# Transformer block on one core: attention inputs (batches 1 to 7) and second-FFN inputs (0 to 6) transposed by VectorE in 32x32 blocks and a DMA hop through DRAM, with new orders of work

## The reference

```python
x = x + 0.5 * ffn(layernorm(x))        # ffn: layernorm * gamma + beta, then a 256x256 ternary weight, + bias
x = x + attention(layernorm(x))        # 16 query heads, 4 key/value heads of 128, rotary embedding,
                                       # causal window of 64, softmax, output projection 2048 -> 256, + bias
x = x + 0.5 * ffn(layernorm(x))        # the same ffn once more
```

## Time and profile before

| | us |
|---|---|
| runs, median of 3 (lowest, highest) | 791.79 (791.75, 793.09) |
| the profiled execution, its own time | 793.39 |
| its span in the trace | 790.5 |

### The profile page before, as it was taken

One profiled execution on the slowest core, in us unless ns is written; L12 is line 12 of the kernel. 1 busy time (PEld: TensorE's weight loads), 2 busy tenths in 40 slices (PEclk: granted clock), 3 DMA queues, 4 the chain that ended last, 5 costly groups with the idle time before them and its releaser, 6 DMA issues.

```text
span 790.5 us, 16087 instructions
## 1 busy us (share of the span) xinstructions
PE 778.3 (98%) x5630; PEld 727.2 (92%) x5630; DVE 626.1 (79%) x1321; ACT 469.6 (59%) x1602; POOL 455.7 (58%) x466
## 2 busy tenths in 40 slices
PE   8999999999999999999999999999999999999997
PEld 7688999999999999999999999999999999999996
DVE  5888967988688877888769887688867988688757
ACT  5366665657646565655747556475664657645574
POOL 3778555766446754567536773476635676446443
PEclk9999999999999999999999999999999999999999
DMA  8572324352252423425153242533224452243410
GB/s 300 114 194 59 90 55 120 95 127 48 55 152 63 121 54 89 126 55 120 41 135 94 68 99 49 134 92 97 67 55 121 94 129 45 57 104 68 107 29 27
DMA packets 54352, 74.10 MB, mean 94 GB/s; under 512 B 7168, under 2 KB 30208, under 8 KB 54272
## 3 DMA queue, kind: packets, MB, share of 16 engines
q1 hardware_dynamic: 53712, 72.74, 37.7%
q10 hardware_dynamic: 560, 0.34, 0.2%
HBM read 14.33 MB, written 4.19 MB: 23 GB/s over the span
## 4 chain that ended last, share of the span: by engine, by line
PE 92%; DVE 3%; POOL 2%; DMA 1%; issue 1%; ACT 0%; SPq 0%; DVEq 0%; POOLq 0%
PE job_p L656 33%; PE attn_p L656 22%; PE scores_p L673 13%; PE heads_p L656 11%; PE probsT_p L737 7%; PE job_p L833 4%; PE job_p L817 2%; POOL q_s L1282 1%; DMA x_res<-wo 1%; POOL probs L1271 1%; DMA x_in<-x 0%; DVE parts L1015 0%; DMA rope_swap<-rope_sin 0%; POOL wo_s L1253 0%; DVE rope_sin L934 0%
## 5 line engine op out<-in xcount | busy, mean ns | idle before, releaser
L656 PE MATMUL attn_p<-wo_s,headsT 128*128 128x256 f32 x1536 | 209.2, 286 | 1.0 <-ACT headsT L1175 0.7
L656 PE MATMUL job_p<-xnT,wq_s 128*128 128x512 f32 x768 | 205.3, 403 | 1.2 <-DVE v_s L951 1.1
L656 PEld LDWEIGHTS attn_p<-wo_s,headsT 128*128 128x128 f32 x1536 | 196.5, 191 | 7.0 <-ACT headsT L1175 1.4
L1154 ACT ACTIVATE probs<-scores_p,neg_max 128x96 f32<-128x96 f32 x512 | 167.6, 352 | 51.8 <-DVE neg_max L900 51.6
L1271 POOL TENSOR_TENSOR probs<-probs,inv_sum 128x384 f32<-128x384 f32 x128 | 107.9, 843 | 152.0 <-DVE inv_sum L906 151.9
L1282 POOL TENSOR_TENSOR q_s<-q_s,rope_swap 128x512 f32<-128x512 f32 x128 | 164.3, 1291 | 52.3 <-DMA rope_swap<-rope_sin 52.2
L1175 ACT ACTIVATE headsT<-heads_p,columns_s 128x512 fp32r<-128x512 f32 x128 | 88.0, 688 | 140.9 <-PE heads_p L656 140.5
L656 PEld LDWEIGHTS job_p<-xnT,wq_s 128*128 128x128 f32 x768 | 135.8, 189 | 26.6 <-DVE v_s L951 1.7
L934 DVE SCALAR_TENSOR_TENSOR rope_sin<-job_p,columns_s,rope_t 128x512 f32<-128x512 f32 x160 | 118.9, 743 | 21.1 <-PE job_p L656 19.9
L673 PE MATMUL scores_p<-k_s,q_s 128*128 128x96 f32 (+2 forms) x1024 | 131.6, 272 | 0.3 <-POOL q_s L1282 0.2
L673 PEld LDWEIGHTS scores_p<-k_s,q_s 128*128 128x128 f32 x1024 | 126.5, 192 | 3.4 <-POOL q_s L1282 1.1
(11 more groups left out here) (96 smaller groups left out, 972.7 us busy)
## 6 DMA issues: line engine op xcount, KB each, us to landing
rope_swap<-rope_sin SPq DMA_DIRECT2D x320, 128.0 KB, 2.3
v_odd<-v_s SPq DMA_DIRECT2D x64, 192.0 KB, 3.3
x_in<-x SPq DMA_DIRECT2D x15, 256.0 KB, 4.2
out<-x_res SPq DMA_DIRECT2D x15, 256.0 KB, 2.5
x_tr<-x_transposed SPq DMA_DIRECT2D x7, 512.0 KB, 5.3
q_s<-wq SPq DMA_DIRECT2D x3, 512.0 KB, 10.1
q_s<-wo SPq DMA_DIRECT2D x2, 512.0 KB, 10.6
x_res<-wo SPq DMA_DIRECT2D x2, 512.0 KB, 4.8
```

What stands on the lines that cost most here:

```text
L656: mm = nc.tensor.matmul(dst, a(p), b(q), start=clears and i == 0, stop=len(pairs) == 1, skip_group_check=True)
L1154: ins = nc.scalar.activation(probs[:, i, k, 0:REACH], scores_p[i][:, k, 0:REACH], ACT.Exp, bias=neg_max[:, i, k:k + 1], accum_out=row_sum[ ...
```

## The change

Fourteen pairs of halves are transposed in another way: XT of batches 1 to 7 and YT2 (written YT..p) of batches 0 to 6. Their `job_p` transposes on TensorE are gone. Instead
- the normalization writes y as runs of 32 elements in another order;
- "turn" (YT2) and "aturn" (XT), one VectorE instruction over 128x1024 float32 in place, transposes every 32x32 block;
- "send" and "asend" on SP copy all of y (512 KB) to a DRAM tensor; "land" and "aland" wait for that, and bring it back by four DMAs of 128 KB into `x_tr`, which puts the blocks on their partitions;
- ScalarE and VectorE make high and low parts from `x_tr` instead of PSUM: for XT one operation of 128x512 per chunk e instead of per half; for YT2 VectorE's low parts are cut into 128 columns.

`x_tr` now has two more tenants per batch, so `loadt` moved behind YT..p. All five tables are written anew. The lines of middle batches around the attention input, and the core of the rest:

```diff
 TENSOR middle
-        W4c T5c S7c K3c O4c Q12c W5c T6c Q13c S8c O5c FO0n W6c T7c
-        S9c Q14c FO1n O6c W7c T8c Q15c S10c O7c W8c XT0n T9c XT1n S11c
-        O8c K0n W9c T10c Q0n S12c O9c W10c T11c V00n S13c Q1n O10c W11c
+        T3c S5c Q9c Q10c O2c W3c FO0p T4c S6c Q11c O3c W4c T5c FO1p
+        O4c S7c K3c Q12c W5c T6c S8c Q13c O5c W6c T7c S9c FO0n FO1n
+        Q14c O6c Q15c W7c T8c S10c O7c W8c T9c O8c W9c S11c T10c O9c
+        W10c S12c T11c S13c K0n Q0n O10c W11c V00n T12c S14c Q1n Q2n O11c
 TENSOR first
+        W6c S8c FO0n T7c FO1n Q14c O6c W7c S9c Q15c T8c O7c W8c S10c
+        O8c T9c S11c W9c T10c O9c S12c W10c T11c S13c K0n O10c Q0n W11c
 VECTOR middle
-        Q12c probsT6c heads5c max8c Q13c YT1n FO0n heads6c max9c inv8c Q14c probsT7c FO1n astats0n
-        astats1n heads7c inv9c probsT8c Q15c max10c XT0n heads8c max11c XT1n inv10c probsT9c K0n inv11c
+        heads15p Q6c probsT0c Q7c evac1p max2c stats1p heads0c K2c max3c turn0p inv2c probsT1c Q8c
+        K3c Q12c inv7c heads5c max8c probsT6c Q13c inv8c heads6c max9c FO0n FO1n astats0n astats1n
+        Q14c probsT7c aturn0n inv9c heads7c probsT8c max10c Q15c heads8c inv10c probsT9c max11c heads9c probsT10c
+        inv11c max12c XT0n inv12c heads10c K0n probsT11c max13c Q0n V00n heads11c inv13c max14c Q1n
 VECTOR first
+        K3c max7c Q12c heads5c inv7c probsT6c Q13c YT1n heads6c max8c FO0n astats0n FO1n probsT7c
+        astats1n inv8c Q14c max9c heads7c aturn0n probsT8c Q15c inv9c max10c heads8c inv10c probsT9c max11c
 SCALAR middle
+        heads6c exp9c probsT7c anorm0n anorm1n mask10c heads7c probsT8c exp10c heads8c probsT9c mask11c heads9c probsT10c
+        exp11c mask12c mask13c XT0n probsT11c exp12c heads10c heads11c mask14c V00n exp13c probsT12c exp14c mask15c
 GPSIMD middle
+        probs7c residual0c center1n ascale0n ascale1n probs8c probs9c K3c Q12c probs10c Q13c Q14c Q15c probs11c
 SYNC middle
-        K1c loadt0n Q4c Q5c Q6c load0n Q7c K2c Q8c Q9c Q10c store0p Q11c store1p
-        K3c shift1c Q12c Q13c Q14c Q15c K0n Q0n Q1n Q2n Q3n shift0n
+        load0n K1c Q4c Q5c Q6c Q7c K2c send0p Q8c land0p Q9c shift1c Q10c loadt0n
+        Q11c store0p store1p K3c Q12c Q13c Q14c asend0n Q15c aland0n K0n Q0n Q1n Q2n
...
+    hop = {kind: nc.dram_tensor("hop_" + kind, (P, BLOCKS * E), F32).ap() for kind in ("XT", "YT2")}
...
+            def send(x):
+
+                sp.wait_ge(y_turned, TURNS[x[0].replace("send", "turn"), *x[1:]] + 1)
+                sp.dma_start(hop[turned_name(x)[0]], y_flat).then_inc(y_sent, 16)
+
+            def land(x):
+
+                kind, _, b = turned_name(x)
+                sp.wait_ge(y_sent, 16 * (SENDS[x[0].replace("land", "send"), *x[1:]] + 1))
+                if kind == "XT":
+                    sp.wait_ge(centered, CENTERED["center", 1, b] + 1)
+                    sp.wait_ge(ln_lo, FFN_IN["YT1", 1, b] + 1)
+                else:
+                    sp.wait_ge(xn_lo, XN["XT", 0, b + 1] + 1)
+                for i in range(4):
+                    sp.dma_start(x_flat[:, i * E:(i + 1) * E],
+                                 hop[kind][32 * i:32 * (i + 1), :].rearrange("a (j f) -> j a f", j=4)).then_inc(landed, 16)
...
+            def turn(x):
+
+
+                first = Y_HALVES[turned_name(x)]
+                for n in (first, first + 1):
+                    wait_y(dve, n)
+                nc.vector.transpose(y_flat, y_flat).then_inc(y_turned, 1)
+
             def xn_low(x):
                 dve.wait_ge(xn_hi, XN[x] + 1)
+                if turned(x):
+                    for e in range(EC):
+                        ins = nc.vector.tensor_tensor(xn_placed(1, e), xn_turned(e), xn_placed(0, e).bitcast(F32),
+                                                      ALU.subtract)
+                    ins.then_inc(xn_lo, 1)
+                    return
...
             def xn_high(x):
+                if turned(x):
+                    wait_landed(act, x)
+                    act.wait_ge(job_ready, last_projection(x[2] - 1) + 1)
+                    for e in range(EC):
+                        ins = nc.scalar.activation(xn_placed(0, e), xn_turned(e), ACT.Copy)
+                    ins.then_inc(xn_hi, 1)
+                    return
```

More of the change, by code:

```diff
@@ L65 @@
     "first": """
[L66 to L72, removed]
+        K1c Q4c Q5c S0c S1c Q6c V10c T0c Q7c W0c S2c T1c O0c S3c
@@ L88 @@
-        S9c Q15c O6c W7c T8c O7c W8c S10c T9c S11c O8c W9c T10c S12c
-        O9c W10c T11c S13c O10c W11c T12c S14c O11c W12c T13c S15c O12c W13c
-        T14c YT0c O13c W14c T15c O14c YT2c W15c FO0c O15c YT3c FO2c FO3c
+        K1c Q4c O13p W14p S0c T15p S1c Q5c V10c O14p W15p Q6c T0c S2c
+        Q7c O15p W0c T1c S3c K2c Q8c O0c Q9c W1c T2c S4c Q10c O1c
+        W2c T3c S5c Q11c V11c O2c W3c T4c S6c FO0p K3c O3c W4c T5c
+        Q12c FO1p O4c W5c S7c T6c S8c Q13c O5c Q14c W6c T7c S9c Q15c
+        O6c W7c T8c O7c W8c S10c T9c S11c O8c W9c T10c S12c O9c W10c
@@ L101 @@
     "first": """
[L102 to L106, removed]
@@ L123 @@
[L123 to L127, removed]
@@ L128 @@
-        norm2c YT0c YT2c heads15c FO0c evac2c stats3c tailb3c YT3c FO2c tailc3c FO3c
+        probsT14p heads13p K1c Q4c max0c probsT15p heads14p evac0p max1c Q5c stats0p inv0c inv1c heads15p
+        V10c Q6c max2c probsT0c Q7c evac1p stats1p heads0c max3c K2c inv2c turn0p inv3c probsT1c
+        Q8c heads1c max4c Q9c probsT2c Q10c probsT3c YT0p heads2c inv4c max5c Q11c V11c probsT4c
+        inv5c YT1p heads3c FO0p K3c max6c heads4c probsT5c inv6c Q12c FO1p max7c heads5c max8c
+        probsT6c inv7c Q13c Q14c inv8c heads6c probsT7c max9c Q15c heads7c probsT8c inv9c max10c heads8c
@@ L139 @@
     "first": """
-        w9f w11f exp0c exp1c mask2c mask3c probsT0c heads0c V10c probsT1c exp2c heads1c exp3c probsT2c
-        mask4c w10f mask5c V11c heads2c exp4c probsT3c mask6c YT0n YT1n w12f probsT4c heads3c exp5c
-        exp6c mask7c heads4c probsT5c mask8c probsT6c heads5c exp7c mask9c exp8c heads6c probsT7c anorm0n heads7c
-        exp9c mask10c probsT8c mask11c XT0n anorm1n heads8c probsT9c XT1n exp10c exp11c heads9c V00n mask12c
-        probsT10c mask13c heads10c probsT11c exp12c mask14c exp13c mask15c heads11c probsT12c heads12c probsT13c exp14c mask0n
@@ L145 @@
-        V01n exp15c mask1n heads13c
+        w10f w11f exp0c exp1c probsT0c mask2c heads0c mask3c V10c w9f exp2c mask4c probsT1c exp3c
+        YT0n mask5c heads1c probsT2c exp4c mask6c YT1n w12f heads2c V11c probsT3c heads3c probsT4c exp5c
+        heads4c exp6c mask7c probsT5c mask8c exp7c heads5c mask9c probsT6c heads6c exp8c probsT7c anorm0n heads7c
+        anorm1n probsT8c mask10c exp9c mask11c heads8c exp10c mask12c probsT9c heads9c exp11c mask13c probsT10c XT0n
+        probsT11c heads10c exp12c probsT12c mask14c heads11c V00n exp13c mask15c exp14c probsT13c heads12c mask0n V01n
@@ L146 @@
+        exp15c mask1n heads13c
     """,
     "middle": """
-        probsT14p heads14p probsT15p exp0c exp1c V10c heads15p probsT0c mask2c norm0p mask3c YT0p exp2c heads0c
-        norm1p probsT1c mask4c exp3c mask5c heads1c probsT2c YT1p exp4c heads2c YT0n V11c probsT3c exp5c
-        mask6c probsT4c heads3c mask7c exp6c probsT5c heads4c mask8c exp7c heads5c probsT6c YT1n mask9c heads6c
-        probsT7c exp8c exp9c heads7c mask10c mask11c probsT8c anorm0n anorm1n XT0n heads8c XT1n exp10c probsT9c
@@ L160 @@
+        probsT7c exp9c heads7c probsT8c mask11c heads8c probsT9c exp10c mask12c exp11c heads9c mask13c probsT10c exp12c
         heads10c probsT11c mask14c exp13c heads11c mask15c probsT12c exp14c heads12c probsT13c exp15c heads13c probsT14c heads14c
```

185 lines of the change are left out of this document (122 added, 63 removed).

## The result

| | us |
|---|---|
| kernel before, median of 6 runs (lowest, highest) | 791.78 (790.75, 793.09) |
| changed kernel, median of 6 runs (lowest, highest) | 834.65 (829.14, 837.25) |
| ratio, 95% interval | 1.0523 (1.05 to 1.0545) |
| profiled execution of the changed kernel | 831.78, span 830.0 |

The sign was right and the size was not: 796.0 was predicted, in 783 to 805. Against the profiled execution of before, 38.4 us are to be explained, or 49.6 with the 11.2 us that TensorE was to save. (The medians lie 42.9 us apart: the profiled execution of before is slower than any of its six runs, that of the changed kernel is one of its faster ones.)

The account below looks back on a forecast made before the run. TensorE, 98% busy, was taken as the bound. Saving 11.2 us but adding 15.0 us of waits (+3.8) took the profiled execution from 793.4 to 797.2 us, the median from 791.8 to about 796; range 783 to 805.

Parts of the forecast that it names:

- the 11.2 us that TensorE was to save: TensorE: 14 removed transpose steps at 0.44 us (XT) plus 14 at 0.36 us (YT2).
- TensorE is the bound, and a step taken from it is worth its distance to the next: TensorE, 98% busy, waits for nobody mid-kernel; each removed step saves its start-to-start distance, 0.44 or 0.36 us.
- Turn 1.2 us: VectorE's 128x1024 transpose takes 1.2 us (ends 0.8 and 2.4); 14 turns are 16.7 us of VectorE.
- W7c 0.7 late, O8c at 12.0 after FO1n's start: TensorE, middle batches: W7c waits 0.7 us for VectorE's probsT7c; O8c starts at 12.0, not 9.9, 2.1 us late.
- 19.7: TensorE, middle batches: K0n's start in us after FO1n's, moved from 17.6 by the 2.1 us wait.
- Send 3.8, landing 5.3, hop 9.1: XT's trip through DRAM in us; lands at 17.3, converted at 18.5, 1.2 ahead of K0n, so hidden.
- The formula: DMA check for the hop: 2.0 us plus bytes over 436 GB/s, giving 3.2 and 2.3 us, 7.5 instead of 9.1.
- rival 3: Hop late, K0n waits for the landing if turn end to landing exceeds 10.4 us; 803 to 810 us; chance 0.13.
- YT..p's hop "about 0, at most 0.5 us": Second-FFN input before FO0p: turn ends 23.5, landing 33, converted 35 and 36.5, FO0p at 36; almost no wait.
- Low parts from two SBUF operands, 0.04 us each and 7 us for the cut, off the path: VectorE: 84 new operations add 3.4 us, YT2's 128-column cut another 7 us, beside its idle time.
- Middle, first and last batches 15.0 us of waits: TensorE waits: 13.2 us in six middle batches, 1.3 in the first, 0.5 in the last.

Follow-up runs that it names:

- e13_yt1n: e11_yt2only with VectorE's YT1n moved behind Q13c and GpSimd's offset1n behind residual0c in the middle batches; 788.24 us.
- e8_noturn: Changed kernel with the hop's send and landing left out and the 14 turns cut to 32 columns each; 813.41 us.
- e1_scatter: Changed kernel with each send as four scattering DMAs of 128 KB and each landing as one DMA of 512 KB; 815.6 us.
- e3_both: e1_scatter with, in middle batches, VectorE's probsT7c ahead of Q14c and ScalarE's heads8c ahead of exp10c; 813.72 us.
- e10_all: e9_bias with e7_order's edits and GpSimd's queue reordered to fit them; 808.49 us.
- e9_bias: e6_heads3 with GpSimd's bias0n and bias1n moved after Q10c and probs6c in the middle batches; 808.53 us.
- e6_heads3: e3_both with VectorE's heads3c ahead of YT1p in the middle and last tables; 811.61 us.
- e11_yt2only: Only second-FFN inputs turned, with scattered sends and one landing; middle tables of e9_bias up to T6c, then of the kernel before; 798.3 us.
- e5_port: Separate kernel: VectorE operations alone and beside GpSimd additions; with two SBUF operands they took 1343 and 1354 ns beside them.
- e12_xtonly: Only attention inputs turned, with scattered sends and one landing; middle tables of the kernel before up to T6c, then of e10_all; 804.66 us.
- e7_order: e6_heads3 with the middle batches' stretch between FO1n and K0n reordered (S11c, S12c, K0n and next-batch xn pieces earlier); 833.03 us.

## Why the prediction was wrong, point by point

- **TensorE is the bound, and a step taken from it is worth its distance to the next.** Right as far as it was measured: e13_yt1n is 4.4 us (2.9 to 6.0) faster for the half that was reckoned at 5.0. For XT's half, reckoned at 6.2, no run shows the gain free of waits.
- **Turn 1.2 us.** Right, 1.24. Its weight in the argument was wrong: without it nothing is won (0.7 us, e8_noturn).
- **W7c 0.7 late, O8c at 12.0 after FO1n's start.** Right in the trace: W7c 0.79, and FO1n's start at 484.70 to O8c at 496.71 is 12.01. Working through the tables with row durations gave this to a tenth. Behind O8c it was short: even where nothing waits for the landing (e1_scatter), K0n comes 20.4 us after FO1n's start and not 19.7, by small waits at O9c, W10c and S12c. And it did not give what remains when the two places are mended: as much again, in smaller waits (e3_both, e10_all).
- **Send 3.8, landing 5.3, hop 9.1.** This step failed. Send 2.6 to 2.8, 1.0 until SP was free to issue, landing 8.3, hop 12.0. I priced the landing by the 512 KB load of the earlier trace rows, whose outermost loop is 128 partitions; this one's is 4. The formula that I took beside it as a check (7.5 us) stands in a section on DMAs issued from GpSimd, while mine were issued from SP; it was further off. K0n came at 21.45 after FO1n's start (506.15 less 484.70), not 19.7. I had the case as rival 3, with 10.4 us as the point of decision, a chance of 0.13 and 803 to 810 us. At K0n the rival's price was right (10.2 us, 1.5 in each of seven batches); by e1_scatter the slow landing costs 19 us, not 7 to 14, as it also took YT..p's room.
- **YT..p's hop "about 0, at most 0.5 us".** This step failed by most, 20.7 us between FO0p and O3c. The turn ended 12.4 us ahead of FO0p, as reckoned (12.5), but the landing came 11.0 us after it instead of 9.5, and the low parts then took 2.15 us, which take 1.34 where GpSimd is away (e9_bias). About half of the 20.7 is the hop's: with the fast landing FO0p is in time, and O3c is still 1.3 us late in most batches (e1_scatter), by the stretched low parts ahead of VectorE's heads3c (e6_heads3).
- **Low parts from two SBUF operands, 0.04 us each and 7 us for the cut, off the path.** The terms were mis-sized and misplaced: `lnT` operations took 31 us more of VectorE, not about 10. The earlier trace rows had the evidence, a maximum of 1051 beside a median of 476, and I averaged it. Nor did it fall on the new operations alone: the 28 of YT..n kept their form and went from a mean of 516 to 869 ns, while XT's 14, with two SBUF operands and no GpSimd instruction beside them, stayed at 689. The wait is not random: it is one GpSimd instruction for each such operation, so it falls where the tables put both together, and whatever stands behind on VectorE carries it to TensorE. Getting two of four such operations out of the way of one step made the difference between 798.3 and 788.2 (e11_yt2only, e13_yt1n).
- **Middle, first and last batches 15.0 us of waits.** Too low, though the least of the misses: XT alone, with a fast hop and 6.2 us of reckoned gain, ends 12 us over the kernel before, so it has some 18 us of waits; both inputs, mended as far as I got, have some 27.

In sums: 834.65 less 19 (landing, e1_scatter), less 7 (the repairs of the order, two of them against the stretch, e10_all), leaves 808.5; the 16 us over the kernel before that remain are, with the gain of 11.2, some 27 us of waits, of which the part between FO1n and K0n is the larger. Why they stay is not shown: each edit removed the wait that it was aimed at and others took its place. That no order of both inputs turned could beat the kernel before is not shown; seven orders did not, and whether an eighth would stays open.

## What to carry to other kernels

Before a transfer is priced by a row of the same size, compare the outermost loop of its pattern with that row's. When an operation moves from PSUM to SBUF operands, list what GpSimd runs in the same microseconds and charge one whole GpSimd instruction for each piece, so cut such work into few pieces and keep it away from GpSimd's additions. In a pipeline where the bound engine never waits, half of a change may pay where the whole does not: here the half whose hop had 12 us of room did (4.4 us, once its order was mended), and the half with 12 us of dependent steps behind it did not.

## What the runs showed of the hardware that I had not expected

- The last of four DRAM-to-SBUF copies of 128 KB in 1 KB packets landed 6.5 us after its issue (90 GB/s for the four together) with an outermost loop of 4; with one of 32 a copy took 2.9 us (270 GB/s).
- A VectorE transpose of 128x1024 float32 in 32x32 blocks takes 1.24 us in place (changed kernel). From one SBUF tensor to another it takes 1.22 us alone and 1.21 beside GpSimd's additions (e5_port); in e12_xtonly six of the seven in place ran partly beside a GpSimd instruction, and all seven took 1.23 to 1.25.
- Some waits of TensorE cost more than themselves. In e7_order it waited 2.6 us for S12c (until 504.83), and the granted clock (the eighth column; stretches of 2 us) then fell to the lower level of 1.2 GHz for some 3 us:

```profile
503.00:505.00 2.00, 0.17 (x2) 0.17 (x2) 0.28 (x1) 2.00 (x10) 1.77 (x2) 1.00 0.00 0
505.00:507.00 2.00, 2.00 (x13) 2.00 (x14) 0.71 (x2) 0.70 (x2) 0.00 (x0) 0.63 0.00 0
507.00:509.00 2.00, 2.00 (x11) 2.00 (x11) 2.00 (x4) 0.00 (x0) 1.18 (x1) 0.52 0.00 0
509.00:511.00 2.00, 2.00 (x15) 1.82 (x14) 0.34 (x1) 0.86 (x4) 0.00 (x0) 1.00 0.00 0
```

O9c, 12 matmuls, took 2.9 us in it instead of 1.7. The granted clock came down to about half in the same way behind each of the six waits of that length in this run, and behind the one of 3.3 us in the changed kernel (last batch, 766 to 768 us). In e11_yt2only it was 0.50 in the 2 us that followed a wait of 2.0 us and the first projection after it; behind the other five waits at this place, of 1.2 to 1.6 us, it stayed at 1.00.
